# Causal attention with heads of 64: the second pair of scores moved directly behind the first

## What is computed

```python
HEAD_DIM, NHEADS, KVHEADS = 64, 32, 8
h = _rms(x, ln_w)
q = (h @ wq).reshape(B, S, NHEADS, HEAD_DIM)
k = (h @ wk).reshape(B, S, KVHEADS, HEAD_DIM)
v = (h @ wv).reshape(B, S, KVHEADS, HEAD_DIM)
q, k = _rope(q, k)
k = jnp.repeat(k, 4, axis=2)
v = jnp.repeat(v, 4, axis=2)
scores = jnp.einsum('bqhd,bkhd->bhqk', q, k) / np.float32(np.sqrt(HEAD_DIM))
scores = jnp.where(causal[None, None], scores, jnp.float32(-1e+30))
attn = jax.nn.softmax(scores, -1)
o = jnp.einsum('bhqk,bkhd->bqhd', attn, v).reshape(B, S, NHEADS * HEAD_DIM)
x = x + o @ wo
```

## Time and profile before

| | |
|---|---|
| median of three runs | 3724.21 us (3715.98 to 3729.96) |
| span of the profiled execution | 3687.3 us, from the first to the last instruction |
| mean granted TensorE clock over the span | 0.938 |
| instructions | 65201 |

### The profile page before, as it was taken

The page is one execution under the profiler, slowest core; times in us unless marked ns, Lnnn a source line. Parts: engine busy times, 40 slices in busy tenths (PEclk is TensorE's granted clock), DMA queues, the critical chain, the costliest instruction groups (busy, mean ns, idle before and its releaser), DMA issues. The chain is left out here.

```text
span 3687.3 us, 65201 instructions
## 1 busy us (share of the span) xinstructions
PE 3303.7 (90%) x22154; PEld 2194.8 (60%) x22154; DVE 2631.0 (71%) x8703; ACT 1933.5 (52%) x5275; POOL 990.3 (27%) x960
## 2 busy tenths in 40 slices
PE   6999999987997899997899999988799749999975
PEld 4666767664554344445667667665455437887853
DVE  5888888885444788873788888887344567777755
ACT  4667767664222366774676767666222125555531
POOL 3211112233454001012121212143444332222213
PEclk8999999998998689997999999998899769999986
DMA  4140500013755322302060500011756300000010
GB/s 129 52 170 7 166 1 1 20 48 110 178 91 116 70 46 58 73 23 72 1 220 1 172 1 1 4 48 57 215 88 122 89 1 15 1 16 4 1 34 23
DMA packets 202239, 234.78 MB, mean 64 GB/s; under 512 B 20662, under 2 KB 188536, under 8 KB 201080
## 3 DMA queue, kind: packets, MB, share of 16 engines
q1 hardware_dynamic: 170968, 190.48, 17.0%
q0 software_dynamic: 30944, 40.14, 6.5%
HBM read 98.13 MB, written 133.73 MB: 63 GB/s over the span
## 5 line engine op out<-in xcount | busy, mean ns | idle before, releaser
L1816 ACT ACTIVATE p_prob<-bank,p_small 128x256 f32<-128x256 f32 (+3 forms) x1280 | 646.2, 515 | 156.0 <-DVE p_small L1988 151.3
L1988 DVE CUSTOM_DVE_ANT_0 bank<-bank,p_mask 128x256 f32<-128x256 f32 (+3 forms) x1280 | 579.0, 490 | 97.1 <-PE bank L1559 85.7
L2336 POOL TENSOR_TENSOR p_tm<-p_rope_a,p_rope_b 128x512 f32<-128x512 f32 x192 | 245.8, 1280 | 1269.0 <-DVE p_rope_b L1968 1264.5
L1559 PE MATMUL bank<-p_k,p_q 64*128 64x256 f32 (+3 forms) x3840 | 529.2, 347 | 13.6 <-ACT p_prob L1816 12.5
L1821 ACT ACTIVATE p_prT<-bank 128x512 f32<-128x512 f32 x752 | 426.0, 601 | 211.5 <-PE bank L1568 209.6
L1568 PE MATMUL bank<-g_ident,p_prob 128*128 128x128 f32 x3008 | 438.3, 284 | 54.4 <-DVE p_prob L1997 20.8
L1997 DVE TENSOR_SCALAR p_prob<-p_prob,p_small 128x256 f32<-128x256 f32 (+3 forms) x1280 | 424.5, 395 | 11.3
L1577 PE MATMUL bank<-p_prT,p_v 128*64 128x512 f32 (+1 forms) x1504 | 428.2, 619 | 0.3 <-ACT p_prT L1821 0.3
L1568 PEld LDWEIGHTS bank<-g_ident,p_prob 128*128 128x128 f32 x3008 | 330.0, 142 | 150.6 <-issue 50.2
L1559 PEld LDWEIGHTS bank<-p_k,p_q 64*128 64x128 f32 (+1 forms) x3840 | 339.1, 188 | 116.1 <-issue 65.1
L2034 DVE TENSOR_REDUCE p_nmax<-bank 128x1 f32<-128x512 f32 x512 | 320.8, 683 | 56.8 <-PE bank L1618 54.6
(11 more groups left out here) (288 smaller groups left out, 6215.8 us busy)
## 6 DMA issues: line engine op xcount, KB each, us to landing
sorted<-p_blank SPq DMA_DIRECT2D x32, 2304.0 KB, 19.2
p_w<-in_L_ffn_w SPq DMA_DIRECT2D x96, 256.0 KB, 4.5
p_h_in<-sorted SPq DMA_DIRECT2D x158, 144.0 KB, 2.7
p_k_st<-k_saved SPq DMA_DIRECT2D x16, 288.0 KB
p_q_st<-q_saved SPq DMA_DIRECT2D x16, 288.0 KB
g_stage<-in_L_ffn_wq SPq DMA_DIRECT2D x8, 512.0 KB, 3.8
g_stage<-in_L_ffn_wo SPq DMA_DIRECT2D x16, 256.0 KB, 4.3
q_saved<-p_qp SPq DMA_DIRECT2D x16, 256.0 KB, 3.2
```

What stands on the lines that cost most here:

```text
L1559: ins = pe.matmul(h.use.ap[:, 0:n], q[rows, at, :], k[rows, kp, o.g, keys], start=i == 0, stop=i == 2)
L1816: act.activation(s.prob.ap[:, 0:s.o.w], s.use.ap[:, 0:s.o.w], ACT.Exp, bias=sm[:, 0, j:j + 1], scale=-1.0, accum_out=sm[:, 1, j:j + 1]).th ...
L1988: dve.tensor_tensor_reduce(x, x, A.mask[:, A.mask.shape[1] - o.w:], -1.0, FAR, ALU.add, ALU.min, o.sm.ap[:, 0, h.j:h.j + 1]).then_inc(made)
```

## The change

The matmuls of both score pairs now stand at the head of a step; the entry that VectorE reads is an entry of its own, `row_maxima`, so that the maxima of heads 2 and 3 can stand elsewhere: behind the low part of the weighted values, ahead of the output product's entry and of the second piece. The exponentials of heads 2 and 3 stand behind that piece, ahead of the transposes. Where `wide` is true, the order stays as it was. No instruction is added or removed.

```diff
             for j in heads:
                 h = Phase()
-                h.o, h.j, h.use, h.prob, h.max_made = o, j, sring.take(), prob.take(), self.vector_made.up()
+                h.o, h.j, h.use, h.prob = o, j, sring.take(), prob.take()
                 s.heads.append(h)
                 o.probs.append(h.prob)
                 o.scored = h.use.full
+            return s.heads
+
+        waiting = []
+
+        def row_maxima(heads):
+            s = self.step("row_maxima", A)
+            s.heads = heads
+            for h in heads:
+                h.max_made = self.vector_made.up()
                 waiting.append(h)
-
-        waiting = []
...
-                scores(cur, *((0,) if wide else (0, 1)))
+                pairs = [scores(cur, 0)] if wide else [scores(cur, 0, 1), scores(cur, 2, 3)]
+                row_maxima(pairs[0])
                 weighed = weigh(full) if full else None
                 if prev:
                     normalise(prev)
...
                 exponentials()
                 if weighed:
                     weighed = low_parts(weighed)
-                if wide:
-                    scores(cur, 1)
+                row_maxima(scores(cur, 1) if wide else pairs[1])
                 if settled:
                     project_out(settled)
                     settled = None
                 route_last()
                 beside()
                 if not wide:
-                    scores(cur, 2, 3)
+                    exponentials()
                 route_last()
                 for kt in range(0, min(2, nturn)):
                     turn(prev, kt)
                 exponentials()
                 if wide:
-                    scores(cur, 2)
+                    row_maxima(scores(cur, 2))
...
                 if wide:
-                    scores(cur, 3)
+                    row_maxima(scores(cur, 3))
                     exponentials()
...
-        elif s.kind == "scores":
-            o = s.o
+        elif s.kind == "row_maxima":
             w.wait_ge(A.masked)
             for h in s.heads:
+                o = h.o
                 x = h.use.ap[:, 0:o.w]
                 w.wait_ge(h.use.full, o.sm.after)
```

## The result

The changed kernel takes **3903.72 us** (median of 4 runs, 3886.36 to 3906.52); measured beside it, the kernel before takes 3727.09 us. The ratio is 1.0464 [1.0437, 1.0490]: by the two medians 176.6 us slower, where I had forecast 108, and 19 us above the upper end of my range (3885). The sign held and so did the waits for banks that I had summed; the size did not.

A forecast was written before the change was run, and what follows sets the result against it. TensorE was taken as the bound, by very little, with VectorE's release of PSUM banks deciding. Regular units +87 us and router units +21 us made +108 on the 3687.3 us span; plus 36.9 gave 3832 us, range 3775 to 3885.

The forecast's parts named there:

- (3,0): Attention step: output's addition stands behind the two second maxima on VectorE, so the third transpose group waits; +1.2 us.
- (3,1): Attention step: transposes wait for the weighted values' low part, then for k's low part behind the maxima; +1.45 us.
- The bank chain: Attention outside the scores: four banks taken in turn, each user waiting for the one four places before it.
- T1 of (3,1): Second transpose group in (3,1), needing the weighing's bank: starts 7.04 us into the step, against 6.35 before.
- (0,1), (1,0), (2,0): nothing waits: Three attention steps with one or two groups of transposes: no waits, so -0.3, -0.1 and -0.3 us.
- the 24 units without the router: Attention units not sharing time with the router: +3.6 us each, 52.9 us for 49.3, +87 us together.
- the eight others: Units at the stages' ends, sharing time with the router: 2.7 us each, between nothing and 5; +21 us together.
- the forecast's bounds of 53 and 150 us: Whole kernel: low, exponentials in time and another term half hidden, 3777 us; high, copies late too, 3874 us.
- my third rival: Regular units' clock also falls to 0.93, up to 3.3 us a unit, 3875 to 3911 us; chance 0.07.
- The 36.9 us between span and median: Whole kernel: median of the runs shown lies 36.9 us above the profiled span; added to reach the forecast.
- The form's gain: Each attention step: joined pairs save a switch between the scores' 64-row form and the other; 0.35 us, bounds 0.22 and 0.4.
- The rival built on it (3634 us): TensorE alone decides: banks back in time, each attention step gains 0.35 us, 90 us in all; chance 0.08.

The follow-up runs named there:

- add_first: Changed kernel with the second pair's maxima put behind the output's addition on VectorE; 3889.03 us, 1.0452 of the kernel before.
- filled: Changed kernel with the first four transposes of (3,1) issued three times instead of once; 3815.37 us (1.0366), run again 3812.16 us (1.0349).
- after_again: The changed kernel unaltered, run again in one set with the filled kernel; 3853.24 us, 1.0463 of the kernel before (first run 3903.72 us).
- pair_max: Changed kernel with the second pair's exponentials put back behind the copies of the first two transposes; 3956.06 us, 1.0617 of the kernel before.
- pair_only: Kernel before with only the second pair's score matmuls moved directly behind the first, maxima and exponentials at their old places; 3936.32 us, 1.0579.
- stagger: Kernel before with each step's second score pair in its old place, directly followed by the next step's first pair; 3713.67 us (0.9970), again 3664.71 us (0.9944).
- before_again: The kernel before, unchanged, profiled a second time; 3728.46 us, 1.0019 of the kernel before.

## Why the prediction was wrong in size

**The steps without the clock.** Measured change per step against forecast, from the windows above and the earlier trace rows:

| step | (0,0) | (0,1) | (1,0) | (1,1) | (2,0) | (2,1) | (3,0) | (3,1) | unit |
|---|---|---|---|---|---|---|---|---|---|
| forecast | +0.3 | -0.3 | -0.1 | +0.4 | -0.3 | +1.0 | +1.2 | +1.45 | +3.6 |
| measured | +0.3 | -0.35 | 0.0 | +0.4 | 0.0 | +1.1 | +1.15 | +1.4 | +3.9 |

The bank chain was right to 0.1 us in the six long steps; T1 of (3,1) starts 7.05 us into the step (7.04 forecast), T3 at 8.64 (8.6), and add_first shows that (3,0)'s term is the place of the addition. Wrong was "(0,1), (1,0), (2,0): nothing waits" for (2,0): its second transposes wait 0.17 us for q's low part, which VectorE starts only at 475.10, behind the scaling:

```profile
475.07 0.60 PE L1575 MATMUL bank<-g_ident,p_prob 128*128 128x128 f32 x4
475.84 0.65 PE L1575 MATMUL bank<-g_ident,p_prob 128*128 128x128 f32 x4 [0.17 <-DVE p_q L1980]
```

**The sum.** The medians of one set split it: the filled kernel, whose regular units have no half clock, is 129.3 us slower than the one before (3812.16 and 3682.89), and the changed kernel another 41.1 us (3853.24). That is 170.4 us in all, and 176.6 in the first result; the two ratios are the same (1.0463 and 1.0464), so the last 6 us are not resolved. The profiled spans (3687.3 before, 3816.1 filled_again, 3847.6 after_again) show where it lies. From before to filled_again it is 128.8 us for 108 forecast: the 24 units without the router 97 (87 forecast), the eight others 27 (21, bounds 0 to 40), the way from the first stage to the second 10 (0 forecast; it is 3 in the run of filled) and the rest -5. That sum lies inside the forecast's bounds of 53 and 150 us.

**The clock** adds 31.5 us by the spans, 24 of them in the 20 regular units, and 41 us by the medians; the mean granted clock of the span is 0.938 before, 0.926 in after_again and 0.939 in filled_again. This is the step that failed: the forecast summed the new waits with the clock at 1.00 throughout and had its fall as my third rival, at a chance of 0.07, in place of the sum, of which the range took only a part. It came on top of the sum. The rival's span, 3875 to 3911 us, holds the result, but in part by luck: it gave the clock 43 to 79 us, and 21 us come from the terms above. The reason I gave against it, that the last regular step idles too at a clock of 1.00, compared 0.36 us of idle time with the 1.4 and 0.5 us that the same forecast had put there. Its price was taken as 7% of all work (up to 3.3 us a unit); it is one stretch of 3.4 us at half speed, 1.0 to 1.7 us in most units with one. The Trainium skill, TensorE: Matmul & The Clock Gate, section A second HAM failure mode, tells of a bf16 kernel that idles briefly between groups of matmuls as it cycles through PSUM banks, and swings between the two clocks; the changed kernel beside the filled one agrees with that. Yet idle time alone does not decide: pair_max has the same 1.42 and 0.49 us there, and more elsewhere, and only two of its regular units fall below 1.00. Nor does the busy share of a unit, by which the rival went: pair_only's is 84% (47.95 of 56.78 us) at 1.00 in all but one, the changed kernel's 89% with stretches at half speed. What else must come together stays open. In after_again the stretches lie 54.6 us apart (276.3 and 330.9 above) and the units with them are 54.7 to 54.9 us long, so it recurs at nearly the same place in each.

**The offset.** The 36.9 us between span and median, which I took as time outside the span, is not that: a run's time is 1.8 us above its span (3906.52 and 3904.7). I had added the change, by steps read from a profile of the faster kind of set, to the median of the slower kind. That did little harm, since the change costs about the same in both: 177 and 170 us by the medians, and in the eight units at the stages' ends 35 us between two profiles of the slower kind (before_again, after) and 31 between two of the faster.

The form's gain, 0.35 us, was right where nothing takes it, in (0,1). The rule of the Trainium skill, TensorEngine Tiling (Array Packing), section Key Properties, agrees with that. The rival built on it (3634 us) did not come, and stagger shows a limit even without the new waits: a unit with next to no wait left gains 0.7 us, not 2.8, and 1.3 us of the difference is taken back at the weighing.

## What to carry to other kernels

Work of the bound engine that stands between two of its uses of a bank, or between a product and the copy that the next product reads, is a cover: before moving it, list for each user of a bank or buffer what covers its release, at the old and at the new place. Where a forecast puts new idle time into TensorE's busiest stretch, price the clock as well, on top of the waits and not as an alternative; a few repeated matmuls inside a wait can be cheaper than the wait. Before summing on one profile, compare it with a second of the same kernel.

## What the hardware showed that I had not expected

In the sets in which the kernel before takes 3724 to 3727 us, the traces have a trait that the others lack. During the router's scatters (indirect DMAs issued by POOL, in the units at the stages' ends) semaphore updates of all engines arrive several us behind the end of their instruction. Counting instructions whose update comes 0.3 to 6 us late, each of the nine profiles of such sets has 157 to 204, and each of the eight others, the first profile of before among them, 0 to 2. Of VectorE's waits of before_again between 700 and 900 us (total, times, longest) these are the two ahead of the maxima; the first, ended by an update to which no instruction's end is near, is not in the trace of before:

```profile
DVE bank L1988 <- remote: 21.1, 8, 4.6
DVE bank L1988 <- PE bank L1559: 16.7, 11, 3.1
```

Whether this lateness is the time difference or only goes with it, and what decides the kind, was not tried. The number of the chip alone does not: sets of both kinds were recorded with chip 6.
